# A transformer block on one core: gate weight prepared in the first stage, the other weights in sixteenths, and projections as half-height matmuls between the score matmuls

## What is computed

```python
x = x + attention(layernorm(x), w_q, w_k, w_v, w_o)
x = x + ffn(layernorm(x), w_gate, w_up, w_down, s_gate, s_up, s_down)

# attention
q, k, v = x @ w_q.T, x @ w_k.T, x @ w_v.T            # split into 32 heads
attn = softmax(q @ k.T / sqrt(16))
out = (attn @ v) @ w_o.T

# ffn, with bitlinear weights
def bitlinear(x, w, scale):
    w_mean = mean(abs(w))
    w_q = clip(round(w / (w_mean + 1e-5)), -1, 1)
    return x @ (w_q * w_mean * scale).T
xq = int4_quant(x)
gate, up = bitlinear(xq, w_gate, s_gate), bitlinear(xq, w_up, s_up)
inter = int8_quant(up * square(relu(gate)))
return bitlinear(inter, w_down, s_down)
```

## Time and profile before

| | before |
|---|---|
| median of 3 runs | 991.39 us (988.03 to 992.25) |
| the profiled execution | 990.27 us |
| its span (first to last instruction) | 988.5 us |
| mean granted TensorE clock, of full | 0.987 |
| PE busy | 928.7 us (94%) |
| DVE busy | 834.2 us (84%) |
| ACT busy | 759.2 us (77%) |
| POOL busy | 157.5 us (16%) |
| mean DMA rate | 66 GB/s |

### The profile page before, as it was taken

The page is one execution under the profiler, slowest core; times in us unless marked ns, Lnnn a source line. Parts: engine busy times, 40 slices in busy tenths (PEclk is TensorE's granted clock), DMA queues, the critical chain, the costliest instruction groups (busy, mean ns, idle before and its releaser), DMA issues.

```text
span 988.5 us, 16486 instructions
## 1 busy us (share of the span) xinstructions
PE 928.7 (94%) x5790; PEld 286.9 (29%) x5806; DVE 834.2 (84%) x1516; ACT 759.2 (77%) x1408; POOL 157.5 (16%) x298
## 2 busy tenths in 40 slices
PE   4799999999999999999999999999889988899997
PEld 3343222222222222222222222222122224444443
DVE  6597999999999999999999999999883237878873
ACT  4322689888888888988999899988886657866664
POOL 3500012111121111212211123111112210112100
PEclk9899999999999999999999999999999999999998
DMA  8310111131021123312232112513340004411000
GB/s 298 94 37 1 33 38 39 34 78 41 23 55 50 48 55 95 96 34 60 76 121 54 38 39 82 121 54 103 114 137 12 12 10 131 137 43 43 33 22 33
DMA packets 38041, 64.90 MB, mean 66 GB/s; under 512 B 3654, under 2 KB 19014, under 8 KB 37702
## 3 DMA queue, kind: packets, MB, share of 16 engines
q1 hardware_dynamic: 37958, 63.85, 22.3%
HBM read 42.27 MB, written 21.23 MB: 64 GB/s over the span
## 4 chain that ended last, share of the span: by engine, by line
PE 71%; ACT 15%; DVE 6%; issue 5%; DMA 2%; SPq 1%; POOL 0%; ACTq 0%; POOLq 0%; DVEq 0%
PE ps L446 21%; PE ps L429 12%; PE ps L385 12%; PE ps L363 8%; ACT PB L773 6%; PE ps L590 6%; PE ps L326 4%; DVE mx L1014 3%; PE ps L638 3%; PE ps L614 3%; ACT PB L857 1%; ACT XV L835 1%; PE ps L412 1%; DVE XV L1108 1%; DMA tu<-wkT 1%
## 5 line engine op out<-in xcount | busy, mean ns | idle before, releaser
L1014 DVE TENSOR_REDUCE mx<-ps 128x1 f32<-128x512 f32 x1024 | 635.4, 683 | 49.8 <-PE ps L385 43.5
L773 ACT ACTIVATE PB<-ps 128x512 f32<-128x512 f32 x1024 | 537.2, 600 | 93.8 <-PE ps L429 93.1
L429 PE MATMUL ps<-QK 50*128 50x512 f16 x1024 | 301.0, 384 | 15.2 <-ACT PB L773 13.9
L385 PE MATMUL ps<-QK 48*128 48x512 f16 x1024 | 303.1, 385 | 10.2 <-issue 5.6
L446 PE MATMUL ps<-PB,Vg 128*32 128x512 f32 x2048 | 274.6, 608 | 1.6 <-ACT PB L773 0.8
L385 PEld LDWEIGHTS ps<-QK 48*128 48x128 f16 x1024 | 75.5, 93 | 206.5 <-DVE mx L1014 175.5
L429 PEld LDWEIGHTS ps<-QK 50*128 50x128 f16 x1024 | 73.0, 93 | 197.1 <-ACT PB L773 148.7
L363 PE MATMUL ps<-XV,wqk 128*128 128x512 f16 x384 | 111.4, 386 | 1.1 <-DVE wmean L951 1.1
L1247 POOL TENSOR_SCALAR nmb<-nm 128x16 f16<-128x16 f32 x32 | 6.6, 206 | 539.1 <-DVE nm L1019 539.1
L590 PE MATMUL ps<-wo,XV 128*128 128x512 f32 x128 | 61.0, 609 | 0.0
L446 PEld LDWEIGHTS ps<-PB,Vg 128*32 128x32 f32 x2048 | 40.4, 108 | 69.9 <-issue 47.7
(11 more groups left out here) (126 smaller groups left out, 654.1 us busy)
## 6 DMA issues: line engine op xcount, KB each, us to landing
parts_d<-spl SPq DMA_DIRECT2D x64, 128.0 KB
att_d<-OS SPq DMA_DIRECT2D x32, 256.0 KB
QK<-parts_d SPq DMA_DIRECT2D x48, 128.0 KB, 4.5
QK<-parts_d SPq DMA_DIRECT2D x16, 256.0 KB, 4.2
XV<-att_d SPq DMA_DIRECT2D x2, 2048.0 KB, 8.6
QK<-rden_d SPq DMA_DIRECT2D x8, 512.0 KB, 7.5
wqk<-x SPq DMA_DIRECT2D x16, 256.0 KB, 3.9
out<-PB SPq DMA_DIRECT2D x16, 256.0 KB, 2.0
```

Of the source, the lines that this page charges most:

```text
L385: nc.tensor.matmul(ps[:, at % S_BANKS, :], QK[rows, sup % 2, 2 * set_ + p, 0, half * HALF + qt * P:half * HALF + (qt + 1) * P], QK[rows, s ...
L429: nc.tensor.matmul(ps[:, tile_bank_of(place), :], QK[rows, sup % 2, 2 * set_ + p, 1, kt * P:(kt + 1) * P], QK[rows, sup % 2, 2 * set_ + p, ...
L773: nc.scalar.activation(PB[:, at % 3, i, :], ps[:, tile_bank_of(tile_place(sup * 4 + step // KEYT, step % KEYT, i)), :], ACT.Exp, scale=exp ...
L1014: nc.vector.tensor_reduce(mx[:, v % 2, idx, kh:kh + 1], ps[:, at % S_BANKS, :], AX.X, ALU.max).then_inc(s_used, 1)
```

## The change

1. **Gate weight in stage 1.** Its four quarters are loaded behind the sixth projection job's parts into memory that is free then: two in QK buffer 1, one in `wo`, one in `PB`. ACT takes the absolute sums behind value copies 3 to 6 and the signs behind value copies 11 to 14; the mean's matmul stands behind value tile 9 on PE, the total and the factor behind score maxima 33 and 41 on DVE, and the four roundings behind the first split of maxima on POOL. SP now issues the auxiliary rows of QK buffer 1 only once the gate's signs are done (`w_tern[0]` at 4), since the raw weight lay there.
2. **Up and down weight in sixteenths.** `act_pieces` puts one piece of 344 or 352 columns behind the first exponential of each of steps 2 to 7. The up weight's sums are in units 14 to 16 and its signs in 18 to 20; the down weight's in 21 to 23 and 25 to 27. Means move to units 17 and 24, the mean's matmul behind the transposed maxima, DVE's factor to step 2, where it also waits for ACT's copy of those rows.
3. **Half-height projections.** A job is 24 matmuls of 64 rows (`pe_half_job`), 12 on rows 0 to 63 and then 12 on rows 64 to 127, all added up in the same bank; they are spread singly or in twos and threes between scores and tiles.
4. **New step orders.** A string for each of the 8 steps sets the order: S and s a score on side 0 and 1, T and t a tile, h a half-height piece, A the product with the values, R means and rows. The scores of a unit run in a new order of sides to suit.
5. `act_sums` moves from behind the third exponential of step 0 to the front of step 1.

```diff
-WEIGHT_LOADS = (13, 18, 23)
-WEIGHT_SUMS = (14, 19, 24)
-WEIGHT_MEANS = (16, 21, 26)
-WEIGHT_ROUNDS = (17, 22, 27)
+ORDER = ("STtsTAhthshs", "htthsThsAsTshR", "hshthsTsTASth", "hsThtSTsASt",
+         "TtShShhhTShStA", "StShThhtSsTA", "tTTssSAthS", "tSThTShStAs")
+HALF_PIECES = 24
+PIECES = 16
+WEIGHT_LOADS = (None, 13, 20)
+WEIGHT_SUMS = (None, 14, 21)
+WEIGHT_MEANS = (None, 17, 24)
+WEIGHT_ROUNDS = (None, 17, 24)
+WEIGHT_SIGNS = (None, 18, 25)
...
+        def pe_half_job(pe, n, m):
+            sup, qk, half = job_of(n)
+            side, c = m // (3 * KT), m % (3 * KT)
+            k, (a, b) = c // 3, PRODUCTS[c % 3]
+            if m == 0:
+                pe_job_free(pe, n)
+            if m == 3 * KT:
+                pe.wait_ge(job_top, n - JOBS_AHEAD + 1)
+            group, rows = sup % SPB, slice(side * SIDE, side * SIDE + SIDE)
+            last = nc.tensor.matmul(ps[:, job_bank(n), :], wqk[rows, qk, a, k, group * P:(group + 1) * P],
+                                    xparts[sup // SPB][rows, b, k, half * HALF:(half + 1) * HALF],
+                                    start=(m == 0), stop=(m == HALF_PIECES - 1))
...
+        def act_pieces(act, at, r):
+            if r < 2:
+                return
+            for w in (1, 2):
+                m = 6 * (at - WEIGHT_SUMS[w]) + r - 2
+                if 0 <= m < PIECES:
+                    act_abs(act, w, m)
+                m = 6 * (at - WEIGHT_SIGNS[w]) + r - 2
+                if 0 <= m < PIECES:
+                    act_ternary(act, w, m)
...
+                if r == 1 and at > 0:
+                    act_sums(act, at - 1)
                 act_exp(act, sup, step, 0)
+                act_pieces(act, at, r)
                 act_exp(act, sup, step, 1)
                 act_exp(act, sup, step, 2)
-                if r == 0 and at > 0:
-                    act_sums(act, at - 1)
                 act_exp(act, sup, step, 3)
...
                 act_value_copy(act, t)
+                if t in (3, 4, 5, 6):
+                    act_abs_gate(act, t - 3)
+                if t in (11, 12, 13, 14):
+                    act_ternary_gate(act, t - 11)
...
+            sp_weight_half(sp, 0, 0)
+            sp_weight_half(sp, 0, 1)
+            sp_max_rows(sp, 0)
+            sp.wait_ge(w_tern[0], 4)
             sp_aux_rows(sp, 1)
-            sp_max_rows(sp, 0)
```

More of the change, by code:

```diff
@@ L265, in item_of, with tile_head @@
         def item_of(k):
[L267 removed]
+            side = SCORE_SIDES[k]
+            c = SCORE_SIDES[:k].count(side)
+            return c // 4, c // 2 % 2, side, c % 2
+        def tile_head(r, i):
+            side = TILE_SIDES[r][i]
+            return 2 * TILE_SIDES[r][:i].count(side) + side
         def tile_place(at, r, i):
@@ L465, in values, with piece @@
                         pe_av(pe, (at * KEYT + r - LATE) // STEPS, (at * KEYT + r - LATE) % STEPS)
-                def pieces(first, end):
+                def piece(m):
                     if job_in(at):
-                        for m in range(first, end):
-                            pe_job(pe, job_in(at), m)
+                        pe_half_job(pe, job_in(at), m)
                 def rows():
@@ new lines, in pe_superunit @@
+                scores, tiles, halves = 0, 0, PIECES_BEFORE[r]
+                for what in ORDER[r]:
+                    if what in "Ss":
+                        score(scores)
+                        scores += 1
+                    elif what in "Tt":
+                        tile(tiles)
+                        tiles += 1
+                    elif what == "h":
+                        piece(halves)
+                        halves += 1
+                    elif what == "A":
+                        values()
+                    else:
+                        means()
+                        rows()
@@ L1288, in pool_superunit @@
                     pool_att(pool, 1)
-                for w in range(3):
+                for w in (1, 2):
                     if at - WEIGHT_ROUNDS[w] in (0, 1):
@@ L1373, in _ @@
             pool_split_max(pool, 0, 0)
+            for q in range(4):
+                pool_round(pool, 0, q)
             own_wait(pool, v_copy, TILES)
@@ L1502, in sp_weight_half @@
             if w == 0:
+                if h == 1:
+                    sp.wait_ge(w_low, 3)
+                    sp.wait_ge(xn_ready, 4)
+                for q in (2 * h, 2 * h + 1):
+                    sp.dma_start(raw(0, q), wgT[q * P:(q + 1) * P, :]).then_inc(raw_in[0][h], 16)
+                return
+            if w == 1:
                 if h == 0:
```

209 lines of the change are left out of this document (76 added, 133 removed).

## The result

The changed kernel takes **980.24 us** (median of 5 runs, 979.65 to 982.34), the kernel before 992.09 beside it (5 runs, 988.03 to 992.85). The ratio is 0.989 [0.987, 0.992]. The forecast was 970, so the time lies in the range of 957 to 983, but the change brought about half of what was forecast, and it landed next to rival A (983). In the profiled execution the span fell from 988.5 to 979.4 us, 9.1 us.

A forecast was written before the change was run, and what follows sets the result against it. PE was taken to bound plain units, with DVE close behind, and ACT the weight units. Terms +2.0 + 0.3 + 2.0 - 6.2 - 14.8 - 4.6 = -21.3 from 990.27 gave 969, as median 970 us; range 957 to 983.

The forecast's parts named there:

- rival A: Stage 2: PE's saving turns into waits, plain units stay at 20.4, weight units at 21.2; total 983 us, chance 0.14.
- Plain units: Units 0 to 13: PE needs 19.85 us, 0.15 more for waits gives 20.0 against 20.44; 6.2 us less in all.
- Units 14 to 25: Up and down weight in small pieces: units fall to what ACT needs, 248.2 us for 263.00, 14.8 less.
- Units 26 to 29: Small signs in units 26 and 27, no half-clock spells: 83.5 us for 88.11, 4.6 less.
- Start: Stage 1 and first tile: 2.0 for absolute sums, 0.3 for small gate work, 2.0 for auxiliary rows; 4.3 us more.
- absolute sums (2.0): Stage 1: the gate's absolute sums on ACT delay tile copies, DVE waits about 1 us four times, partly covered; 2.0 us more.
- the rows (2.0): Start of stage 2: auxiliary rows wait for the fourth gate sign, so PE's first tile waits for them; 2.0 us more.
- act_sums: Moving this 0.6 us copy to step 1's front costs nothing, covered before step 1's values start.
- B: Stage 2: DVE's floor is reached, plain units 19.5 us, weight units 20.0; total 952 us, chance 0.12.
- C: PE's instruction supply, 70 ns each, binds: a unit of 312 instructions takes 21.9 us; total 1011 us, chance 0.06.
- D: Half-height pieces never run beside a score: 2.1 us more, units of 22.1; total about 1013 us, chance 0.03.
- two signs that would prove me wrong: Marks above 20.4 us in units 1 to 13, or a first tile after 116 us.

The follow-up runs named there:

- e4_crossing: The changed kernel with step 3 reordered, a tile and a score more between the last piece on rows 0 to 63 and the first on 64 to 127: 978.7 us.
- e7_abs: e6_aux with the gate's absolute sums moved behind the copies of the transposed tiles and ahead of value copies 4 to 7: 971.78 us.
- e1_weights_only: The changed kernel's weight schedule alone, with full-height projections, step orders and act_sums place of the kernel before: 976.54 us.
- e11_hybrid: The changed kernel with edits of e4_crossing, e5_alternate, e6_aux and e7_abs; half-height pieces only in units 0 to 12, full-height projections and old orders after: 970.33 us.
- e9_sums: The changed kernel with act_sums back behind the third exponential of step 0: 988.67 us.
- e2_max_half: The changed kernel with every row maximum taken over 256 of its 512 columns, the rest left out: 968.88 us, one run.
- e5_alternate: The changed kernel with the scores of units 0 and 1, in stage 1, on the alternate sides of the kernel before: 979.43 us.
- e6_aux: e1_weights_only with the first tile waiting only for QK buffer 0's auxiliary rows, buffer 1's waited for in superunit 1: 974.26 us.

## Why the prediction was half right

**Plain units: wrong, and this is most of the miss.** "PE then needs 19.85 us" failed, and so did "0.15 more than PE's own time". Forecast 6.2 us less, measured 0.3 more over units 1 to 13. Three things lead from 20.0 to 20.47. The walk had a rule for the sides but none for the seam: the kernel lets the pieces of the second row group start only once the first group's have ended, 0.17 (e4_crossing won 0.149 of it). It also had no tile banks: the tile at 275.90 waits 0.19 more than a place. And the waits that come with full maxima were 0.43, not 0.15. Together that is 0.64; the other six stretches took 0.17 less than my sum. Before, PE's own time and these waits were 20.09 + 0.35; after, 20.04 + 0.43. I had written that waits were 0.38 with 1.0 of room and then took fewer of them with 0.4 of room; the bound of 20.44, "all of the saving gone in waits", was the value to take. Rival A said this, with the right mechanism in the main (banks that do not even out the strings; it did not have the seam) and 0.14 of chance. That the total still lies in the range of 957 to 983 says little for the forecast, since the range reached up to A.

By the Trainium skill (TensorE: Matmul & The Clock Gate, on the span model) a pair costs 0.220 us, an estimate from the page's figures. In after, the pieces that start at 258.99, 259.22, 259.43, 259.65 and 259.87 stand 0.22 apart, so here the trace agrees with the page better than with my 0.23, which I had read from one pair of before. It changes little: with 0.22 a place the sum is 19.4, six stretches of the kernel with short maxima agree with it to 0.07, and stretches 3 and 7 are 0.23 and 0.26 over.

**Units 14 to 25: right mechanism, 3.4 us too much.** -11.4 for -14.8. Blocks of 1.33 are gone; PE itself, which in before sat idle 0.70 us for an exponential ten times in these units, has no idle time over 0.3 us left in them. Units with six sixteenths take 21.0 (forecast 20.8), with four 20.78 (20.2), with the mean 21.15 (21.0). The first kind is near ACT's own sum, 18.1 + 6 x 0.47 = 20.9; a sixteenth costs ACT 0.47 us from its start to the next exponential (448.92 to 449.39) where I had 0.43. The step that failed is "four: 3 x 20.2": ACT's sum is 20.0 there, but such a unit can't fall below the plain one, which I had at 20.0 and which takes 20.47. It is the first error carried on.

What the sixteenths add to a plain unit lies in the short stretches between values. In after, stretch 6 takes 2.08 for 1.79 in every unit with pieces, and stretch 8 takes 1.93 for 1.75 in units with six (PE's timelines, worked out). In unit 15 stretch 6 runs from 436.32 to 438.41, and PEld's timeline shows a tile and the values waiting for exponentials:

```profile
437.87 0.09 PEld L483 LDWEIGHTS ps<-QK 50*128 50x128 f16 x1 [0.40 <-ACT PB L780]
...
438.41 0.16 PEld L500 LDWEIGHTS ps<-PB,Vg 128*32 128x32 f32 x8 [0.42 <-ACT PB L780]
```

A stretch with three places is 1.77 us by my rule, less than the 1.9 that four exponentials take here, and behind a sixteenth ACT has no idle time to catch up in. With the full-height orders two projection matmuls stand in this stretch, which takes 2.61 with and without sixteenths, and the three kinds of unit take 20.7, 20.6 and 21.25. In the unit with the mean 0.48 of the 0.68 over a plain unit lie in stretch 2, where the mean's matmul stands. Short maxima take 0.13, 0.05 and 0.57 off the three kinds, so DVE counts in the units with the mean and hardly in the others. No run moved a sixteenth or a tile within these orders, so this is read from traces and not tried.

**Units 26 to 29: right.** -4.6 for -4.6 from the products with the values (-4.9 by the marks); units 27 and 28 are 2.5 and 2.4 shorter, and the clock from 699 to 703 us is 1.00 for 0.57.

**Start: two terms near, two missed.** 4.3 forecast, 6.1 measured (6.9 by the mark, of which 0.8 is the copy's new place): 3.1 for scores of one side in stage 1, 1.4 for the rest of the later last value copy, in the main the absolute sums (e7_abs won 1.6), 1.2 for the auxiliary rows (the first tile stands 2.05 behind the last value copy for 0.83), 1.5 for the clock, less 0.4 for a first value copy that is earlier and 0.7 for a shorter unit 0 (from the first tile to the start of its last product with the values 21.38 in before and 20.63 in e4_crossing, both without a spell). The absolute sums (2.0) and the rows (2.0) were near, though my working of the rows adds up to 110.0 and not 109.7; DVE waits 0.93, 0.90 and 0.90 for the tile copies. The missed term was in the diff: the "new order of sides" also orders the scores of stage 1. The step "stage 1's other value tiles are set by PE" should have led there: whatever PE gets more of, they take. Of the aux wait I had written what is late next (SP's rows), but not that PE, idle meanwhile, can come back at half clock.

**Units 30 and 31: no term in the sum.** They take 1.3 us more with the half-height orders, in every kernel that has them there, and none in e1_weights_only or e11_hybrid. No run shows which part of the orders costs it.

**act_sums: priced at nothing, worth 8.4 us.** This is no part of the miss, since the change made the move; without it the change would be worth almost nothing (0.998 [0.997, 1.000]). The forecast compared the new place with the values of step 1; the old one stood before the last exponential of step 0, for which the values of step 0 wait. In the old orders that had room, in the new ones not.

**Rivals B, C and D fell.** DVE's floor was not reached in after. PE took 385 matmuls and 383 loads in 50 us, 65 ns each, for the 70 that C had as the limit. Pieces run beside scores.

Of the two signs that would prove me wrong, one came: marks of 20.47. The first tile was at 113.08, inside, but 5.3 us later than before rather than 4. The failed step in one line: PE's own time in a plain unit was 20.04 and not 19.85, and the waits behind full maxima were 0.43 and not 0.15, so that the 6.2 us did not come.

## What to carry to other kernels

When matmuls of half the rows are woven between others, count places by side and by bank: where the kernel makes a second row group that adds up into the same bank wait for the first one's end, put other work in that seam. When the engine next in line has less than half a microsecond of room in a unit, take the waits of before as a floor for the waits after, whatever the engine's own sum says (here 0.35 became 0.43). Extra work on an engine that feeds the values shows in the shortest stretch between them, not in its sum over the unit. A schedule made for the steady part (an order of sides, a copy's place) also runs in the first stage and in the last units; price it there separately, or let it hold only where it wins. And when an instruction serves as a mark, ask first whether the change has moved it.

## What the runs showed of the hardware that I had not expected

Places with a matmul on either side stand 0.22 us apart, but the two pieces at the seam, on different row groups and adding up in the same bank, start 0.43 apart, with a wait of 0.34 for the first one's end shown on the weight load. The kernel asks for that wait itself (`job_top`); no run left it out, so these runs do not show what the chip would do without it.

A short idling of PE can cost more than itself. In after PE is busy 2.33 of 4 us from 110 us on, and from 114 to 118 the granted clock is 0.64, a mean over its two levels; unit 0 then takes 24.04 us from its first tile to its mark. The kernel e4_crossing has the same instructions up to there, the same wait of 1.55 ahead of the same tile and as idle a PE, but no such spell, and takes 22.56:

```profile
110.74:114.74 4.00, 2.34 (x13) 0.61 (x11) 3.05 (x7) 1.20 (x3) 0.47 (x3) 1.00 0.03 8
114.74:118.74 4.00, 3.86 (x30) 1.00 (x31) 3.34 (x6) 3.43 (x8) 0.92 (x3) 1.00 0.01 2
```

With the same wait e9_sums has no spell either and e2_max_half has one, so these traces do not say when it comes. Likewise unit 28 takes 21.8 us in after and 23.0 in e5_alternate, and 22.9 in e1_weights_only and 24.2 in e6_aux, pairs whose instructions there are the same, with one spell more in the second of each. So differences of 1 to 2.5 us between such kernels can come from the clock alone, and the marks of plain units, the same to 0.01 in thirteen units, tell small edits apart where whole runs cannot.
